# A two-layer graph convolution on one core: tile 1 prepared like the later tiles, first rows sent kind by kind, filler products, scaling on GpSimd, the last position turned

## What is computed

```python
h = jnp.maximum(_layernorm(x, axis=-1), 0.0)
# _ngcf_conv(x, W1, W2, src, dst, n), twice, with relu between:
deg_out = jnp.clip(segment_sum(ones, src), 1.0)
deg_in  = jnp.clip(segment_sum(ones, dst), 1.0)
norm = rsqrt(deg_out[src] * deg_in[dst])
msg = (h[src] @ W1 + h[src] * h[dst] @ W2) * norm[:, None]
out = h @ W1 + segment_sum(msg, dst)
# the result is x + conv(relu(conv(h)))
```

## Time and profile before

| | |
|---|---|
| median of 3 runs | 508.75 us (507.77 to 510.15) |
| the profiled execution: device time, span | 506.1 us, 504.4 us |
| granted TensorE clock, mean | 0.993 of full |
| opening | 0 to about 22.3 us |
| counting | about 22.3 to 185.8 us |
| scaling and the first three positions | 185.8 to about 199.5 us |
| positions 3 to 97, and the last stores | about 199.5 to 504.4 us |

### The profile page before, as it was taken

The page is one execution under the profiler, slowest core; times in us unless marked ns, Lnnn a source line. Parts: engine busy times, 40 slices in busy tenths (PEclk is TensorE's granted clock), DMA queues, the critical chain, the costliest instruction groups (busy, mean ns, idle before and its releaser), DMA issues.

```text
span 504.4 us, 19900 instructions
## 1 busy us (share of the span) xinstructions
PE 484.3 (96%) x8018; PEld 458.6 (91%) x8018; DVE 422.3 (84%) x1092; ACT 249.7 (50%) x706; POOL 139.1 (28%) x376
## 2 busy tenths in 40 slices
PE   5889999999999979999999999999999999999994
PEld 5768888888888869999999999999999999999993
DVE  6999999999999957877777777777988888888883
ACT  1299999999999964433333333332111111111110
POOL 3412434334346301433333333332111111111110
PEclk9999999999999998999999999999999999999998
DMA  3258313021202000000000000000000200010000
GB/s 69 79 102 97 66 28 83 23 73 33 58 15 54 3 1 3 4 1 3 3 3 2 4 3 3 4 1 3 4 3 2 45 3 1 3 44 1 14 18 18
DMA packets 24791, 12.32 MB, mean 24 GB/s; under 512 B 21024, under 2 KB 23376, under 8 KB 24701
## 3 DMA queue, kind: packets, MB, share of 16 engines
q1 hardware_dynamic: 23997, 9.04, 9.2%
q0 software_dynamic: 672, 2.01, 1.4%
q10 hardware_dynamic: 32, 0.01, 0.0%
HBM read 6.21 MB, written 4.05 MB: 20 GB/s over the span
## 4 chain that ended last, share of the span: by engine, by line
PE 88%; ACT 4%; DVE 4%; DMA 2%; issue 1%; SPq 0%; DVEq 0%; ACTq 0%
PE diff L1039 35%; PE slab L951 19%; PE iota_bank L1039 17%; PE diff L933 9%; ACT hots L1076 3%; PE diff L1010 2%; PE diff L1017 1%; PE slab L988 1%; DMA los<-in_dst_dram 1%; PE turn_t L988 1%; PE diff L1006 1%; ACT words L1084 1%; PE iota_bank L1017 1%; PE slab L1039 1%; DMA mixed<-rows 1%
## 5 line engine op out<-in xcount | busy, mean ns | idle before, releaser
L694 DVE TENSOR_TENSOR los<-mixed,iota_bank 128x5120 bf16<-128x5120 bf16 x49 | 137.5, 2809 | 5.2 <-PE slab L951 4.6
L951 PEld LDWEIGHTS slab<-hots,los 128*128 128x128 bf16 x2352 | 119.5, 98 | 13.6 <-ACT hots L1076 0.6
L951 PE MATMUL slab<-hots,los 128*128 128x98 fp8e5 x2352 | 125.4, 209 | 0.2 <-ACT hots L1076 0.2
L1076 ACT ACTIVATE hots<-diff 128x784 f16<-128x784 f32 x147 | 118.4, 848 | 6.3 <-PE diff L933 6.2
L1039 PE MATMUL diff<-late,mixed 128*128 128x128 f16 x1616 | 104.4, 219 | 0.0
L1039 PEld LDWEIGHTS diff<-late,mixed 128*128 128x128 fp8e4 x1616 | 98.7, 99 | 0.4
L1039 PE MATMUL diff<-los,mixed 128*128 128x129 f16 x1470 | 95.6, 220 | 0.0
L576 POOL TENSOR_TENSOR work<-work,h 128x64 f32<-128x64 f32 x98 | 31.5, 321 | 228.2 <-DVE work L811 228.2
L1039 PEld LDWEIGHTS diff<-los,mixed 128*128 128x128 fp8e4 x1470 | 89.3, 98 | 0.3
L933 PE MATMUL diff<-select,mixed 80*128 80x392 f16 x294 | 65.2, 329 | 3.2 <-ACT hots L1076 2.4
L740 DVE TENSOR_SCALAR mixed<-words 128x400 int32<-128x400 int32 x192 | 61.1, 358 | 0.0
(11 more groups left out here) (177 smaller groups left out, 535.1 us busy)
## 6 DMA issues: line engine op xcount, KB each, us to landing
x_sb<-in_x_dram SPq DMA_DIRECT2D x4, 384.0 KB
rows_table<-rows SPq DMA_DIRECT2D x6, 252.0 KB, 2.5
mixed<-rows_table SPq DMA_DIRECT2D x18, 84.0 KB, 2.9
out_dram<-x_sb SPq DMA_DIRECT2D x8, 128.0 KB
los<-in_dst_dram SPq DMA_DIRECT2D x1, 750.0 KB
p_table<-p_rows_sb SPq DMA_DIRECT2D x20, 28.0 KB
p_table<-p_rows_sb SPq DMA_DIRECT2D x20, 7.0 KB
out_dram<-x_sb SPq DMA_DIRECT2D x4, 80.0 KB
```

What stands on the lines that cost most here:

```text
L694: nc.vector.tensor_tensor(out=los[:, b % LOS_RING].rearrange("e s (v t) -> e s v t", t=2), in0=key, in1=val, op=ALU.is_equal).then_inc(los ...
L951: ins = nc.tensor.matmul(to, los[:, u // 2 % LOS_RING, u % 2 * ULOWS + low], pairs, start=(step == 0), stop=(step == USTEPS - 1), skip_gro ...
L1076: nc.scalar.activation(bass.AP(to.tensor, to.offset, [to.ap[0], [step, 2], [STEPS * BLOCKS, 8], [1, BLOCKS]]), diff[m % 2][:, :, 0:HALF].r ...
```

## The change

It does eight things.

- **Opening.** `prev_i` is loaded by ACT's queue, the weights wait for `dst`, ACT makes `samples`, GpSimd clears half of `stack`, and DVE's order is changed: `offset` is made early, both `later` before the second `chosen`. The begins of tiles 1 to 5 come from one comparison and one reduction in place of five counts. GpSimd issues one indirect DMA on trial (`tried`) ahead of the real ones.
- **First rows.** Rows of kinds 0, 1 and 2 of tile 0 are each sent when made, on SP's and ACT's queues.
- **Tile 1** is decoded by GpSimd and sent by SP through DRAM, like tiles 2 to 6, with x loaded after it. PE's turn and ACT's `save_keys` of tile 1 are gone, and DVE's `decode_early(1)` becomes `weigh(1)`.
- **Pairs.** Before unit u stand two pairs more than needed for u below 8, three below 16, then four.
- **Idle products**: 24, 26 and 56 in the opening, and 34 more after the last unit.
- **Scaling.** GpSimd scales pieces 1, 3, 5 and 7, and DVE makes the high half of piece 0.
- **Last position.** Position 97 is computed turned (features by nodes), so that its sums need no turn: DVE scales them and multiplies them with a turned h, two products with stacked weights follow, and the node's own term is added ahead. The check's reduction goes before its comparison, and its product moves from q = 23 to q = 45 of position 97.
- **Last stores** go half to SP's and half to ACT's queue.

The core of the diff (semaphore declarations and the renumbered waits are left out):

```diff
-    TURN_AFTER = {3: 1}
-    KEYS_AFTER = {4: 1}
+    DECODE.update({1: (1, 3), 2: (1, 4)})
+    WEIGH_BESIDE = {2: 1, **{u0 // 2 + 5: t for t, u0 in BEGIN.items()}}
+    SCALED_BY_POOL = (1, 3, 5, 7)
+    def made(u):
+        return min(pairs_of(u) + 2 + min(u // 8, 2), UNITS * STEPS // 2)
     def pairs_beside(u):
-        first = 3 * (u // 2) + 4
-        return [m for m in ((first, first + 1) if u % 2 == 0 else (first + 2,)) if m < UNITS * STEPS // 2]
+        return range(made(u - 1) if u else 0, made(u))
...
         def _(sp):
+            sp.wait_ge(early_rows_ready, 1)
+            for j in range(2):
+                sp.dma_start(stack[0:16, 0, j], rows[16 * j:16 * j + 16, 0]).then_inc(first_in[j], 16)
             sp.wait_ge(rows_ready, 1)
+            sp.dma_start(stack[64:80, 0, 0], rows[0:16, 2]).then_inc(first_in[0], 16)
...
             for t in range(1, TILES):
+                save_p(t)
+                if t == 1:
+                    save_rows(t)
+                turn_keys(t)
+                if t > 1:
+                    save_rows(t)
...
         def _(pool):
+            nc.gpsimd.indirect_dma_start(
+                out=fine[1][0:GRAIN, 0], out_offset=None, in_=src_rows,
+                in_offset=bass.IndirectOffsetOnAxis(ap=row_0[:, 0:1], axis=0)).then_inc(tried, 16)
+            nc.gpsimd.memset(stack[0:96, 1], 0.0).then_inc(consts, 1)
...
+            for step in range(3):
+                decode(1, step)
...
+            pool.wait_ge(rdo_ready, 1)
+            for i in SCALED_BY_POOL:
+                qs = slice(*PIECES[i])
+                nc.gpsimd.tensor_tensor(out=scaled[:, qs], in0=h[:, qs],
+                                        in1=rdo_sc0[:, qs].unsqueeze(2).to_broadcast([128, qs.stop - qs.start, D]),
+                                        op=ALU.mult).then_inc(scaled_by_pool, 1)
...
         def _(dve):
+            def find_begins():
+                v(nc.vector.tensor_tensor(out=junk[:, 1:6], in0=windows[1][:, :, 0:SAMPLES],
+                                          in1=group0[:, 1:6].unsqueeze(2).to_broadcast([ROWS, 5, SAMPLES]), op=ALU.is_lt))
+                v(nc.vector.tensor_reduce(out=before[:, 1:6], in_=junk[:, 1:6], axis=AX.X, op=ALU.add))
+                count_before(6, windows[2][:, 0])
...
             scaled_piece(0)
-            for i in range(1, len(PIECES)):
+            high_piece(0)
+            low_piece(0)
+            for i in (2, 4, 6):
                 scaled_piece(i)
                 low_piece(i - 1)
+                low_piece(i)
             low_piece(len(PIECES) - 1)
...
                 if n == POSITIONS - 2:
+                    dve.wait_ge(own_ready, 1)
+                    v(nc.vector.tensor_tensor(out=x_sb[:, BLOCKS - 1], in0=x_sb[:, BLOCKS - 1], in1=own_ps, op=ALU.add))
...
                 if n == POSITIONS - 1:
+                    dve.wait_ge(acc_ready, n + 1)
+                    nc.vector.tensor_scalar(s_t, bank(n)[:, 0:128], unscale1[:, 0:1], None,
+                                            ALU.mult).then_inc(last_ready, 1)
+                    dve.wait_ge(h_t_saved, 1)
+                    nc.vector.scalar_tensor_tensor(product_t, bank(n)[:, 0:128], unscale1[:, 0:1], h_t,
+                                                   ALU.mult, ALU.mult).then_inc(last_ready, 1)
...
         def _(pe):
-            keep_running(28)
-            turn(0)
-            keep_running(90)
+            keep_running(26)
+            turn()
+            keep_running(56)
...
             pe.wait_ge(los_ready, BLOCKS)
+            keep_running(34)
...
+                    if n == POSITIONS - 1:
+                        ins = nc.tensor.matmul(bank(n)[:, 0:128], parts1[:, q, 0:2 * D], tiles[home(n)][:, q],
+                                               start=(q == 0), stop=(q == BLOCKS - 1))
...
-            turn_pair(POSITIONS - 1)
-            weigh(POSITIONS - 1)
+            nc.tensor.matmul(turn_z[n % 2][:, 0:D], s_t, wt_twice[:, 0], start=True, stop=False)
+            pe.wait_ge(last_ready, 2)
+            nc.tensor.matmul(turn_z[n % 2][:, 0:D], product_t, wt_twice[:, 1], start=False, stop=True).then_inc(z_ready, 1)
...
         def _(act):
+            for s in range(2, 4):
+                part, n = node_rows(out, s, BLOCKS - 1, BLOCKS)
+                act.dma_start(part, x_sb[32 * s:32 * s + n, BLOCKS - 1:BLOCKS]).then_inc(y_out, 16)
```

More of the change, by code:

```diff
@@ L229, in fast_path @@
     rdi_h = spread[:, 0]
+    beside = mixed[:, 2 * Q * 64:2 * Q * 64 + 1024].bitcast(FP32).rearrange("p (i c) -> p i c", i=4)
+    h_t, s_t, product_t = [beside[:, i] for i in range(3)]
+    wt_twice = beside[:, 3].rearrange("p (k f) -> p k f", k=2)
     w0_scaled = words_late[:, 1024:1024 + D]
@@ L445, in _ @@
                     load_x()
+            sp.wait_ge(deg_ready, 1)
+            for k in range(2):
+                for half in range(2):
+                    sp.dma_start(wt_twice[half * D:(half + 1) * D, k], weights[2 + k]).then_inc(w_in, 16)
             for b0, b1 in STORES:
                 sp.wait_ge(y_ready, b1)
-                for s in range(4):
+                for s in range(4 if b1 < BLOCKS else 2):
                     part, n = node_rows(out, s, b0, b1)
@@ L666, in decode_early @@
-                v(nc.vector.scalar_tensor_tensor(rows[:, 0].bitcast(U16), place, 8 * 2048.0, place, ALU.is_le, ALU.mult))
-                v(nc.vector.tensor_tensor(out=shared, in0=shared, in1=own, op=ALU.mult))
-                v(nc.vector.scalar_tensor_tensor(rows[:, 1], q_i, -float(MID), rows[:, 0], ALU.add, ALU.mult))
+                dve.wait_ge(fine_in[0][1], 16)
+                v(nc.vector.tensor_scalar(place_wide, targets, offset[:, 0:1], 2048.0, ALU.add, ALU.mult))
+                v(nc.vector.scalar_tensor_tensor(rows[:, 0].bitcast(U16), place, 8 * 2048.0, place, ALU.is_le, ALU.mult))
@@ L669, in decode_early @@
+                nc.vector.tensor_tensor(out=shared, in0=shared, in1=own, op=ALU.mult).then_inc(early_rows_ready, 1)
+                dve.wait_ge(early_rows_ready, 1)
+                nc.vector.scalar_tensor_tensor(rows[:, 1], q_i, -float(MID), rows[:, 0], ALU.add,
+                                               ALU.mult).then_inc(early_rows_ready, 1)
+                dve.wait_ge(early_rows_ready, 2)
                 nc.vector.scalar_tensor_tensor(rows[:, 2], q_i, -float(MID), rows[:, 1], ALU.add,
@@ L1086, in save_words @@
                                      ACT.Copy).then_inc(slab_saved, 1)
+            act.dma_start(prev_i[1:SROWS], bass.AP(dst.tensor, dst.offset + ROWLEN - GRAIN,
+                                                   [[ROWLEN, SROWS - 1], [1, GRAIN]])).then_inc(prev_in, 16)
             act.wait_ge(dve_steps, 1)
             nc.scalar.activation(root_of_one[:], ones[:], ACT.Sqrt)
-            save_keys(0)
+            act.wait_ge(dst_in, 32)
+            nc.scalar.activation(samples[:, 0:SAMPLES], dst_i[:, GRAIN - 1:ROWLEN:GRAIN], ACT.Copy).then_inc(samples_ready, 1)
+            save_keys()
             act.wait_ge(stack_zeroed, 1)
+            act.wait_ge(early_rows_ready, 2)
+            for j in range(2):
+                act.dma_start(stack[32:48, 0, j], rows[16 * j:16 * j + 16, 1]).then_inc(first_in[j], 16)
             act.wait_ge(rows_ready, 1)
-            act.dma_start(stack[32:48, 0, 0], rows[0:16, 1]).then_inc(first_in[0], 16)
-            for m in range(4):
-                save_weights(m)
+            act.dma_start(stack[64:80, 0, 1], rows[16:32, 2]).then_inc(first_in[1], 16)
             for u in range(UNITS):
@@ L1166, in _ @@
             save_layer(3)
-            for n in range(TOGETHER + 2, POSITIONS + 1):
+            for n in range(TOGETHER + 2, POSITIONS):
+                if n == POSITIONS - 2:
+                    act.wait_ge(h_turned, 1)
+                    nc.scalar.activation(h_t, h_turn_ps, ACT.Copy).then_inc(h_t_saved, 1)
                 save_t(n - 1)
```

233 lines of the change are left out of this document (124 added, 109 removed).

## The result

| | before | after |
|---|---|---|
| median, 12 runs each on one chip | 508.41 us (507.10 to 510.15) | 510.07 us (508.22 to 511.26) |
| the profiled execution: device time, span | 506.1, 504.4 us | 509.12, 507.4 us |
| granted clock, mean | 0.993 | 0.984 |
| first pair starts | 22.31 | 22.48 |
| unit 8, unit 16 start | 40.92, 53.90 | 41.17, 55.42 |

The changed kernel takes 1.003 times the time of the kernel before, 95% interval 1.0016 to 1.0044. That is 1.66 us by the medians, and within 0.5%. The forecast was a gain of 8.1 us. They differ by 3.03 us, 1.4 more than the medians, mainly because the profiled execution of the kernel before took 506.1 us, less than any of its twelve runs beside the changed kernel.

A forecast was written before the change was run, and what follows sets the result against it. The prediction took PE to bound the kernel and looked for places where PE waits or runs slowly. Gains of 1.5, 2.3, 2.4 and 1.9 sum to 8.1 us, taking 508.75 to 500.7 us, range 498.0 to 505.0.

The forecast's parts named there:

- term 1: Opening: sooner counts, gather and first rows bring the first pair to about 20.8, 1.5 us gained, bounds 0.8 and 1.9.
- term 2: First units: fewer early pairs and no tile 1 stop on PE, 2.3 us gained, bounds 0.8 and 2.7.
- term 3: Scaling: idle products hold PE's clock and GpSimd takes four pieces, 2.4 us gained, bounds 0.4 and 2.6.
- 0.4 lost: Opening: the decode waits to about 14.8 if the trial DMA does not take the first-use cost away.
- the clock falls in the opening: Rival: PE's clock falls around the first pair, costing 2.0 us, so 502.7 us; chance 0.15.
- The step through the two queues: First units: PE and ACT work stepped in the new order, starting unit 6 at 34.5 instead of 37.6.
- the pace does not change: Steady part of counting: two units keep taking 3.24 us, all of it PE's products.
- GpSimd and DVE block each other: Rival in the scaling: the two engines hold each other up, giving back 1.3 to 2 us, so 502.4; chance 0.13.
- 4. End: Last position and stores: check's wait, tail and stores gain, turned h costs; 1.9 us gained, bounds 1.1 and 2.6.
- Tile 1, costed at nothing: Tile 1's decode and transfers on GpSimd and SP stay hidden: keys by about 38, wanted at 39.9.
- The rival in which SP's queue makes the kernel slower: Tile 1's keys, rows and x behind one queue land late and delay PE, up to 511.5 us; chance 0.05.
- no change: Rival: scaling clock falls, ACT paces the first units, the end gains nothing; 505.7 us or a little more; chance 0.07.

The follow-up runs named there:

- e1: The changed kernel with VectorE clearing all of `stack` and GpSimd clearing nothing: 504.66 us, 0.9978 of the kernel before.
- f1: The changed kernel with VectorE clearing `stack`, no GpSimd share in the scaling, and 90 idle products before the first pair: 502.35 us, 0.9869 of the kernel before.
- g3: g0 with the check's product back at q = 23 of the last position: 501.46 us, 0.9916 of the kernel before.
- e3: The changed kernel without GpSimd's share in the scaling; VectorE scales all pieces, the 34 idle products stay: 503.94 us, 0.9968 of the kernel before.
- e4: The changed kernel with 90 idle products in place of 56 ahead of the first pair: 505.29 us, 0.999 of the kernel before.
- g0: f1 with the lead kept at two pairs for all units: 500.34 us, 0.9905 of the kernel before.
- g2: g0 without the 34 idle products after the last unit: 502.05 us, 0.9923 of the kernel before.

## Why the prediction was wrong

Three steps failed: the opening's sum left out GpSimd's clear of `stack` (term 1), the pairs put off to units 8 and 16 were priced as PE's work alone, without the wait for ACT (term 2), and VectorE and GpSimd were taken as hardly in each other's way in the scaling (term 3). The clock's fall in the first units came on top.

**1. Opening (+1.5, measured -0.17).** One operation was missing from the sum: `stack`'s half-clear on GpSimd is nowhere in it. Without it L660 takes 0.18 in place of 2.98 us (e1), and the first pair is at 20.65 in e1, where 20.8 was forecast. That agreement is in part luck: up to the last begins e1 gains 0.65 (15.30 to 14.65) of the 0.85 forecast, and behind them 1.0 where 0.6 was forecast. (In f1 to g3 it is at 20.73 to 20.94, at the end of the 90 idle products.) The pieces: comparison and reduction take 0.68 and 0.67 (0.6 each taken). The trial DMA, which was to take most of the 0.98 us ahead of the first gather away, leaves 0.86, and the "0.4 lost" set against it did not come either.

The Trainium skill's page SBUF — State Buffer (section Who interferes with whom) says that the port pair shared by VectorE and GpSimd is an exclusive lock. The trace agrees as far as L660 ends 0.04 us after GpSimd's clear; that it began 0.59 us ahead of the clear and did not finish is left open. The prediction asked this of the scaling and not of the opening.

**2. First units (+2.3, measured -3.78).** Three things, of which the traces give the sizes.
- *The rival "the clock falls in the opening" came true*, in this profile and in three others with 56 idle products. The forecast gave it 0.15 and 2.0 us; it cost 1.5. Its evidence "against" (this gap is shorter than 2.64) was the weak step: gaps of 1.44 to 1.64 us followed by sparse work were enough in four executions. The gap alone does not decide it: e3's was 1.70 and its clock stayed.
- *The rises of the lead.* The prediction paid 0.66 us of PE for the pairs left out. Each rise costs 1.2 to 1.3 (once 1.7, at unit 16 in f1), since the third pair waits for ACT's 0.84 us save, as the chain shows at both. The step through the two queues was right as far as it went: with the clock at 1.00 (e4), unit 6 starts 12.2 us after the first pair, as forecast. It stopped there, ahead of both rises.
- *After unit 16* the prediction said that the pace does not change. It lost 2.3 us in steps at fixed units, in some executions only. Their cause is open, and the change is not shown to bring them: the 2.3 us are in the stage table, since the profile of the kernel before has none, but probably not in the ratio.

With the clock held and on a chip without these steps (e4), the stretch from first pair to end of counting is 162.30 us against 163.32 before: a gain of 1.0. With the rises gone too (g0) it is 161.71, although PE there loses 1.2 us to late rows (2.10 and 2.72 for units 26 and 40, 1.79 without).

**3. Scaling (+2.4, measured -0.97).** The clock half of the step was sound: 34 idle products hold the clock while VectorE keeps its pieces, and are worth 1.56 us (g2; 1.53 against the kernel before in e3), not 2.5. The estimate ran 147 products without a gap in 8.4 us; in e3 they take 8.9, with two waits of 0.27 us for pieces besides, of which its row shows one. The other half failed, by the rival "GpSimd and DVE block each other", which had 0.13. It was priced at 1.3 to 2 us; e3 measures 2.5. It costs more than its price because PE's 1.75 us wait for the second piece brings back the low clock that the idle products had prevented. The bounds held a gain in every case, 0.4 at least, and the stage got slower: the low bound took the clock as fallen and the pieces at most a little late, not VectorE's pieces at twice their time and GpSimd's at 1.19 us instead of 0.94. The Trainium skill's page GPSIMD Engine Reference (section Specifications), which the prediction weighed, spoke against this part, and the trace agrees by 1.36 against 0.62.

**4. End (+1.9, measured +1.89).** Position 3 to the last `x_sb` went from 301.07 to 299.74 (1.33 gained), and the stores behind it from 3.89 to 3.33 (0.56). The parts: the check's wait was forecast at 1.2 and g3 shows 1.36, 1.6 with what it does to the tail; the shorter tail, forecast at 0.8, is 0.85 (from the last product's start to `x_sb`, 3.00 to 2.15). What these two leave of the 1.33 gained puts the turns of h and the own product at about 0.9, an estimate, where 0.8 was forecast. No part was far off, so this term did not come out by luck.

**Tile 1, costed at nothing, cost nothing.** SP issued the transposing DMA at 37.47 and x from 41.45 to 49.96; no `los` waited for keys, and VectorE first used x at 54.35. But the keys landed at 41.60, after the 39.9 at which the prediction had VectorE ask for them; they did not hold it only because VectorE came to block 7 as late as 44.05. In g0, which has neither the clear nor the rises nor a low clock there, keys at 38.27 and block 7 at 40.21 are what was forecast. The rival in which SP's queue makes the kernel slower did not occur for tile 1. Its mechanism appeared elsewhere, in g0 to g3, for tile 3.

The outcome, no change, had a chance of 0.07, and 510.07 us lies 5 us above the range and 4 above the 505.7 that this rival itself was priced at. The rivals of clock and blocking were taken one at a time. Both happened, along with an operation that was not priced.

## What to carry to other kernels

Before giving idle GpSimd a share, list what VectorE runs in that same stretch, however small: one held instruction on the path costs the whole length of GpSimd's. Idle products bridge a wait only so far: here 34 of them kept the clock through a wait of 0.75 us and not when one of 1.75 followed, and 90 in place of 56 kept it in the opening but ran into the first pair. When work is shifted to start sooner, step the queues through to the end of the shift; here the lead's rises and then the next tile's rows took back what the start had gained. The best version that ran keeps the changed opening, pairs and end, but clears `stack` on VectorE, scales on VectorE, has 90 idle products and a constant lead of two: 0.9838 (0.9809 to 0.9868) and 0.9905 (0.9886 to 0.9923) of the kernel before in two comparisons.

## What the runs showed of the hardware

- A VectorE instruction that takes 0.18 us without a GpSimd clear of 2.35 us beside it took 2.98 and ended with the clear, although that instruction reads one small tensor only.
- Two streams of two-tensor operations slowed each other down: GpSimd's pieces of 448 elements went from 0.94 us to 1.19, VectorE's from 0.62 to 1.36.
- The granted clock fell to 0.50 after gaps of 1.44 to 1.64 us and sparse work behind them in four executions, and did not in a fifth, with the same instructions there as after and a gap of 1.70.
- The first indirect gather started 0.86 us after its address with a trial gather ahead of it, and 0.98 and 1.01 without.
